# Cross attention: key and value sides made behind the first memory layer, scores in four banks

## The chip, the cores and the metric

The kernel runs on one core of a Trainium2 chip. The metric is the device time in microseconds from start to end of one execution; lower is better. TensorE is PE, VectorE is DVE, ScalarE is ACT, GpSimd is POOL, SyncE is SP.

## What is computed

Four batches of 256 tokens (width 256) pass four layers in a row: L0, a gated cross attention over a 1601 x 128 context with 16 heads of 64, and a GELU feed-forward; L1, a memory layer (attention over the same context, then a sigmoid gate and an RMS norm); L2, self attention, cross attention and an MLP; L3, a memory layer like L1. The part that the change touches is the cross attention of L2, 16 heads of 8:

```
cq = heads(rms_norm(hidden_states, ln_post_cross_w) @ cq_w, NH, CHD)
ck, cv = jnp.split(encoder_outputs @ ckv_w, 2, axis=-1)     # 1601 x 128 each, no dependence on x
cctx = sdpa(cq, heads(ck), heads(cv), causal=False)         # softmax(q k / sqrt(8)) v
hidden_states = hidden_states + cctx @ cdense_w
```

## The kernel before

The engines run written-out instruction streams, ordered by semaphores; there is no scheduler. Each engine loops over the four batches. Inside a batch: L0 pair by pair of heads, its output projection and feed-forward, `memory_layer(0)`, self attention, cross attention, MLP, `memory_layer(1)`. PE takes its instructions strictly in program order, so a wait ahead of one holds back all behind it.

PSUM has eight banks: `X[0]` and `X[1]` of two banks each, `ST[0]`, `ST[1]`, `PV`, `MI`. The 1664 padded keys are 13 tiles of 128 (`KT`), or two halves of 832 (`HALF`), each read as two pieces of 416 (`QUART`).

Cross attention of a batch. PE makes the queries in `MI`, then the keys of all heads in `X[0]` and `X[1]` (twice six matmuls of 416 columns; a factor is split into a high and a low part in fp32r). DVE splits queries and keys into high and low parts (`ck_hi`, `ck_lo`), clears the two `cq_blocks`, and writes the queries of a group into them (`queries`, L1462). The 16 heads go in four groups of four. For a group, `cross_stacks` (L1013, PE) spreads the four heads' keys over the partitions with a constant matrix, in `X[0]` and `X[1]`, and ACT (`keys`, L571) copies them to `ck_stack`, of which there are two. `cross_max` (L1030 on PE, L1472 on DVE) computes all scores of the group a first time, half a row at a time in `X[0]` or `X[1]`, 16 parts, and DVE reduces each to its maximum. The maxima of a row are negated, transposed by PE (`cross_shifts`) and written by DVE into four rows of `cq_blocks`, so that the second computation of the scores comes out shifted. That second one is the loop over the 13 key tiles: two scores matmuls of 512 columns into `ST[0]` and `ST[1]`, two exponentials on ACT into four slots of `probs` (L604), and `pv` (L1062), four matmuls of 32 output partitions, one tile behind. The stacks and the maxima of the next group lie between these on PE:

```
for kt in range(KT):
    for u in range(2):
        n = 2 * kt + u
        pe.wait_ge(pc_exp.handle, pc_exp.at(i, max(0, n - 1)))     # the exponential two back
        ...                                                        # scores n -> ST[n % 2]
    if gr < 3 and kt == 0:
        cross_stacks(gr + 1, 0); cross_stacks(gr + 1, 1)
    if gr < 3 and 1 <= kt < KT - 1:
        for n in range(...): cross_max(gr + 1, n)
    if kt:
        pv(kt - 1)
pv(KT - 1)
if gr < 3:
    cross_shifts(gr + 1)
```

Group 0 has no scores to lie beside: its 16 parts run alone, with the values (`cross_v`, L1001, 39 matmuls of 128 columns into `ST`, copied by ACT to `v_cross`) between them. `transposed(3)` sends 24 matmuls without a use (`WARM`, into `ST[0]`) ahead of the transposes that open self attention.

## Time and profile before

| | us |
|---|---|
| median of 3 runs (lowest, highest) | 2669.77 (2669.46, 2673.37) |
| the profiled execution, its own time | 2673.19 |
| its span, first to last instruction | 2671.4 |
| PE busy | 2186.9 (82% of the span) |
| DVE busy | 1571.4 (59%) |
| ACT busy | 851.5 (32%) |
| POOL busy | 467.8 (18%) |
| granted clock of PE, mean, as a share of 2.4 GHz | 0.887 |

A batch takes about 665 us. In the first one, L0 runs from 40 to 290 us, cross attention from 443 to 591 us. The timeline has one line for one or several equal instructions: start, length, engine, source line, operation, output and inputs, and in brackets how long the engine had been idle and who released it. L625 is PE's helper for every matmul and L1146 is DVE's for two-input operations, so the tiles' names tell the steps apart.

### The profile page before, as it was taken

To read this page: it belongs to the slowest core of one execution; us is meant where nothing else is said; L and a number is where in the kernel's file an instruction comes from. 1 tells how busy PE (TensorE), PEld (TensorE's weight loads), DVE (VectorE), ACT (ScalarE), POOL (GpSimd) and SP (SyncE) were. 2 spreads that over 40 slices of the span, in tenths; PEclk is the share of its full clock that TensorE was granted. 3 is DMA by queue.
4 is the path that set the end of the run, shared out by engine and by line. 5 is a ranking of instruction groups with operands and counts; after the bars stand their busy time and mean duration, and the time that the engine had idled before them with its cause. 6 is when DMAs were issued, how large, how long until landed. Compare 5 with 4: busy or idle time off the path is not lost.

```text
span 2671.4 us, 38462 instructions
## 1 busy us (share of the span) xinstructions
PE 2186.9 (82%) x12780; PEld 1616.3 (61%) x12780; DVE 1571.4 (59%) x2513; ACT 851.5 (32%) x1530; POOL 467.8 (18%) x412
## 2 busy tenths in 40 slices
PE   4999877888599978788859998868876999776987
PEld 3777665546477666554747766655464776665545
DVE  6777346653677735665377772566437776356643
ACT  2444111441244412044124441205412453120531
POOL 2444010000244401000034440100003443010000
PEclk7999887899699988799969998869896999986988
DMA  3000101001000010100100001010010000101000
GB/s 154 13 4 32 67 1 71 1 1 40 26 13 4 32 67 1 71 1 1 40 30 9 4 32 68 1 71 1 1 40 30 9 4 32 67 1 71 1 1 5
DMA packets 15567, 74.61 MB, mean 28 GB/s; under 512 B 2096, under 2 KB 3760, under 8 KB 11952
## 3 DMA queue, kind: packets, MB, share of 16 engines
q1 hardware_dynamic: 14256, 68.90, 6.9%
q10 hardware_dynamic: 1152, 3.67, 0.3%
q8 instruction: 90, 1.47, 0.2%
q14 instruction: 69, 0.57, 0.1%
HBM read 71.51 MB, written 1.05 MB: 27 GB/s over the span
## 4 chain that ended last, share of the span: by engine, by line
PE 72%; DVE 17%; issue 7%; ACT 3%; DMA 1%; POOL 0%; DVEq 0%; SPq 0%; ACTq 0%; POOLq 0%
PE x L625 26%; PE st L625 22%; PE pv L625 18%; PE mi L625 4%; DVE rstd_work L1146 1%; DVE prob_sums L1429 1%; DVE max_parts L1249 1%; PE x L646 1%; DVE k_hi_lo L1146 1%; DVE recip_sum L1300 1%; DVE cq_blocks L1484 1%; DVE rstd_work L1205 1%; ACT probs L510 1%; ACT k_hi_lo L468 1%; DVE max_parts L1476 1%
## 5 line engine op out<-in xcount | busy, mean ns | idle before, releaser
L510 ACT ACTIVATE probs<-st 128x512 f32<-128x512 f32 x416 | 229.6, 596 | 385.3 <-PE st L625 380.6
L1476 DVE TENSOR_REDUCE max_parts<-x 128x1 f32<-128x832 f32 x256 | 253.6, 1021 | 107.9 <-PE x L625 106.2
L1249 DVE TENSOR_REDUCE max_parts<-x 128x1 f32<-128x832 f32 x256 | 258.5, 1016 | 54.6 <-PE x L625 53.2
L604 ACT ACTIVATE probs<-st 128x512 f32<-128x512 f32 x416 | 226.4, 596 | 184.0 <-PE st L625 180.8
L625 PE MATMUL st<-q_hi_hi,k_hi_lo 128*128 128x256 f32 x832 | 236.9, 315 | 29.0 <-ACT v L476 14.3
L433 POOL TENSOR_TENSOR prob_sums<-prob_sums,probs 128x512 f32<-128x512 f32 x160 | 205.8, 1286 | 249.7 <-ACT probs L510 249.7
L625 PEld LDWEIGHTS st<-q_hi_hi,k_hi_lo 128*128 128x128 f32 x832 | 160.7, 193 | 104.2 <-issue 68.4
L625 PE MATMUL pv<-probs,v 128*64 128x256 f32 x1664 | 223.3, 393 | 0.0
L625 PE MATMUL st<-q_lo_shift,k_hi_rows 128*128 128x256 f32 x832 | 213.1, 287 | 0.0
L397 POOL TENSOR_SCALAR k_hi_rows<-probs,const_cols 64x1664 fp32r<-64x1664 f32 x16 | 26.4, 1660 | 991.0 <-DVE probs L1213 990.6
L1146 DVE TENSOR_TENSOR prob_sums<-prob_sums,probs 128x512 f32<-128x512 f32 (+1 forms) x168 | 155.1, 923 | 76.1 <-ACT probs L530 44.0
L625 PE MATMUL st<-cq_blocks,ck_stack 128*128 128x512 f32 x416 | 162.3, 466 | 32.1 <-DVE cq_blocks L1484 30.3
L625 PE MATMUL x<-ck_stack,cq_blocks 128*128 128x416 f32 x512 | 153.6, 416 | 29.1 <-DVE cq_blocks L1143 13.6
L1146 DVE TENSOR_TENSOR k_hi_lo<-x,k_hi_lo 64x832 fp32r<-64x832 f32 x128 | 130.9, 1023 | 73.6 <-ACT k_hi_lo L468 71.7
L625 PEld LDWEIGHTS st<-q_lo_shift,k_hi_rows 128*128 128x128 f32 x832 | 162.1, 195 | 0.0
L625 PE MATMUL x<-k_hi_rows,q_hi 128*128 128x416 f32 x512 | 144.0, 398 | 14.4 <-DVE max_parts L1249 12.0
L625 PEld LDWEIGHTS pv<-probs,v 128*64 128x64 f32 x1664 | 101.0, 137 | 77.2 <-ACT probs L510 24.3
L625 PEld LDWEIGHTS x<-ck_stack,cq_blocks 128*128 128x128 f32 x512 | 106.6, 221 | 62.0 <-issue 31.7
L625 PEld LDWEIGHTS st<-cq_blocks,ck_stack 128*128 128x128 f32 x416 | 68.5, 194 | 118.4 <-ACT probs L604 80.8
L646 PE MATMUL x<-const_f,x_normed 128*128 128x128 f32 x80 | 20.4, 405 | 145.9 <-DVE x_normed L1181 97.8
L625 PE MATMUL pv<-probs,v_cross 128*32 128x256 f32 x1664 | 138.6, 391 | 0.0
L468 ACT ACTIVATE k_hi_lo<-x 64x832 fp32r<-64x832 f32 x128 | 110.2, 861 | 26.5 <-PE x L625 24.0
(260 smaller groups left out, 4408.6 us busy)
## 6 DMA issues: line engine op xcount, KB each, us to landing
w_gate_up<-in_wgu SPq DMA_DIRECT2D x4, 3072.0 KB, 10.3
w_pair<-in_w SPq DMA_DIRECT2D x32, 256.0 KB, 2.6
w_ff<-in_w SPq DMA_DIRECT2D x8, 1024.0 KB, 5.8
w_qk<-in_wqk SPq DMA_DIRECT2D x4, 2048.0 KB, 8.9
w_down<-in_wdn SPq DMA_DIRECT2D x4, 1536.0 KB, 13.6
w_dense<-in_wd SPq DMA_DIRECT2D x4, 1024.0 KB, 12.2
mask_ints<-in_mask SPq DMA_DIRECT2D x4, 832.0 KB, 4.5
ctx_t_raw<-in_ctxT SPq DMA_DIRECT2D x4, 832.0 KB, 6.3
```

Source lines behind the costliest of these rows:

```text
L433: pool.tensor_tensor(acc[:, 0], acc[:, 0], prob[:, (2 * n + 2) % 4], ALU.add)\
L468: act.activation(t["kst"][0:64, h, j * HALF:(j + 1) * HALF].rearrange("p (c n) -> p c n", c=2), X[j][64 * h:64 * h + 64, :].rearrange("p ( ...
L510: act.activation(prob[:, kt % 4], ST[kt % 2][:], ACT.Exp, scale=HD0 ** -0.5).then_inc(p_exp.handle, 1)
L604: act.activation(prob[:, n % 4], ST[n % 2][:], ACT.Exp, scale=float(HC2) ** -0.5)\
L625: return pe.matmul(out, lhsT, rhs, start=start, stop=stop, skip_group_check=True)
L646: last = pe.transpose(X[0][:, o:o + P], src[:, t, ch * P:(ch + 1) * P], ident)
L1146: return dve.tensor_tensor(out, x, y, op)
L1205: link(dve.scalar_tensor_tensor(y, w, 1.5, y, ALU.add, ALU.mult))
L1249: dve.tensor_reduce(mxs[:, qt, h, half:half + 1], X[half][:].rearrange("p (c n) -> p c n", c=2)[:, :, 0:QUART], AX.XY, ALU.max).then_inc(m ...
L1300: dve.reciprocal(rec[:], PV[:, NT:2 * NT]).then_inc(recip.handle, 1)
L1429: link(dve.reciprocal(part, sums))
L1476: dve.tensor_reduce(mxs[:, qt, h, half:half + 1], X[half][:].rearrange("p (c n) -> p c n", c=2)[:, :, 0:QUART], AX.XY, ALU.max).then_inc(m ...
```

## The change

What it does, in the order of a batch:

- Behind the first memory layer PE makes the keys (`cross_k`), the values (`cross_v`) and the stacks of all four groups (`cross_stacks`, now in pieces of 512 columns, up to column 1602). ACT copies the keys twice (`ck_hi` and a full copy `ck`), POOL subtracts one from the other (`ck_lo`), ACT copies values and stacks. There are four `ck_stack` tiles. PE waits for all these copies before `transposed(3)`. The 24 filler matmuls there go.
- The weight `w_ckv` is loaded and split once, ahead of the loop. POOL clears `cq_blocks` and sets the padding columns; ACT writes the queries into `cq_blocks`.
- The maxima are computed by single banks of 512 columns: three per head and query tile, and one of 66 columns for four heads, 26 parts in place of 16. Group 0 takes four banks in turn, the others the two of `X[0]`.
- The scores use four banks (`ST[0]`, `ST[1]` and both of `X[1]`), the exponentials eight slots (`probs`, `probs_cross`). `pv` comes two key tiles at a time behind four scores. The shifts of the next group come ahead of the last `pv` calls. The values lie 16 columns apart, not 32.

PE's order behind the first memory layer, before (`x`, `mi`, `st`, `pv` are the PSUM tiles; out<-in, columns; REGISTER_ALU and ISA rows belong to waits):

```order
L625 MATMUL mi<-w_gate,mc_t 128x256 x2
L625 MATMUL st<-const_r 128x512 x24
L642 REGISTER_ALU
L646 MATMUL x<-const_f,x_normed 128x128 x4
L888 ISA
L625 MATMUL x<-x_v_t,w_qk 128x256 x2
```

And now, from the last stack (`cross_stacks(3, 1)`) on:

```order
L685 MATMUL x<-ck_hi,const_r 128x512
L685 MATMUL x<-ck_hi,const_r 128x258
L685 MATMUL x<-ck_lo,const_r 128x512
L685 MATMUL x<-ck_lo,const_r 128x258
L986 REGISTER_ALU
L702 REGISTER_ALU
L706 MATMUL x<-const_f,x_normed 128x128 x4
L991 ISA
L685 MATMUL x<-x_v_t,w_qk 128x256 x2
```

The filler gave way to the key, value and stack matmuls, whose last four are shown; the wait for the copies (L986) now stands ahead of the transposes.

PE's loop of a group with the next group's maxima, before: one key tile and the next.

```order
L625 MATMUL st<-cq_blocks_143,ck_stack_147 128x512
L1037 REGISTER_ALU
L625 MATMUL x<-ck_stack_148,cq_blocks_144 128x416 x2
L1037 REGISTER_ALU
L625 MATMUL x<-ck_stack_148,cq_blocks_144 128x416 x2
L625 MATMUL pv<-probs,v_cross 32x256 x4
L1077 REGISTER_ALU
L625 MATMUL st<-cq_blocks_143,ck_stack_147 128x512
```

The same place now:

```order
L685 MATMUL x<-ck_stack_156,cq_blocks_150 128x512
L1112 REGISTER_ALU
L685 MATMUL x<-ck_stack_156,cq_blocks_150 128x512
L685 MATMUL x<-cq_blocks_149,ck_stack_155 128x512
L1112 REGISTER_ALU
L685 MATMUL x<-ck_stack_156,cq_blocks_150 128x512
L685 MATMUL x<-cq_blocks_149,ck_stack_155 128x512
L1112 REGISTER_ALU
L685 MATMUL x<-ck_stack_156,cq_blocks_150 128x512
L685 MATMUL pv<-probs,v_cross 32x256 x8
L685 MATMUL st<-cq_blocks_149,ck_stack_155 128x512
```

Scores (`x` or `st` from `cq_blocks`) and single parts (`x` from the next `ck_stack`) alternate, and eight `pv` matmuls stand in a block where four stood. The diff, cut:

```diff
-WARM = {1: 12, 3: 24, 4: 12, 5: 12}
+WARM = {1: 12, 4: 12, 5: 12}
...
-        ks2 = [place(f"ck_stack{s}", [P, SK], F32R, e) for s in range(2)]
-        e = [max(c[0], e[0])]
+        ks2 = [place(f"ck_stack{s}", [P, SK], F32R, k) for s in range(4)]
+        vx = place("v_cross", [P, KT, (H2 + 1) * VXW], F32, k)
...
+            return X[k // 2][:, k % 2 * 512:k % 2 * 512 + 512]
+            return half_bank(m % (4 if gr == 0 else 2))
+            return (ST[0][:], ST[1][:], half_bank(2), half_bank(3))[n % 4]
+            return prob[:, n % 8] if n % 8 < 4 else prob2[:, n % 8 - 4]
...
+                pool.wait_ge(wo_mm.handle, wo_mm.at(b))
+                for n, (dst, value) in enumerate(((vx[:], 0.0), (vx[:].rearrange("p k (h d) -> p k h d", d=VXW)[:, :, :, HC2:HC2 + 1], 1.0))):
+                    pool.memset(dst, value).then_inc(vx_init.handle, 1)
...
+                for j in range(2):
+                    pool.wait_ge(kn_read.handle, kn_read.at(b, j + 1))
+                    pool.sem_inc(passed.handle, 1)
+                    c = slice(j * HALF, (j + 1) * HALF)
+                    pool.tensor_tensor(knl[:, c], knf[:, c], r32(knh[:, c]), ALU.subtract).then_inc(kn_low.handle, 1)
...
+                for k in range(2):
+                    pool.memset(r32(qb2[k][:]), 0.0).then_inc(qb_init.handle, 1)
...
+                def cross_k(j):
+                    act.wait_ge(ck_mm.handle, ck_mm.at(b, j + 1))
+                    x, c = X[j][:].rearrange("p (c n) -> p c n", c=2)[:, :, 0:QUART], slice(j * HALF, (j + 1) * HALF)
+                    act.activation(knh[:, c].rearrange("p (c n) -> p c n", c=2), x, ACT.Copy)
+                    act.activation(knf[:, c].rearrange("p (c n) -> p c n", c=2), x, ACT.Copy).then_inc(kn_read.handle, 1)
...
+                def cross_keys(gr, j):
+                    act.wait_ge(ks_mm.handle, ks_mm.at(b, 2 * gr + j + 1))
+                    n = HALF if j == 0 else S2 - HALF
+                    act.activation(ks2[gr][:, j * HALF:j * HALF + n], X[j][:, 0:n], ACT.Identity, bias=ck[:, K_OH_CROSS:K_OH_CROSS + 1])\
+                        .then_inc(ks_read.handle, 1)
+                act.wait_ge(vx_init.handle, vx_init.at(b))
+                cross_k(0)
+                cross_k(1)
+                cross_v(0)
+                cross_v(1)
+                for gr in range(4):
+                    cross_keys(gr, 0)
+                    cross_keys(gr, 1)
+                    if gr < 2:
+                        cross_v(gr + 2)
...
-                    for kt in range(KT):
-                        for u in range(2):
-                            n = 2 * kt + u
-                            act.wait_ge(sc_mm.handle, sc_mm.at(i, n + 1))
-                            act.wait_ge(pvc_mm.handle, pvc_mm.at(i, max(0, n - 3)))
-                            act.activation(prob[:, n % 4], ST[n % 2][:], ACT.Exp, scale=float(HC2) ** -0.5)\
-                                .then_inc(pc_exp.handle, 1)
-                        if gr < 3 and kt == 0:
-                            keys(i + 1, gr + 1, 0)
-                            keys(i + 1, gr + 1, 1)
+                    for n in range(2 * KT):
+                        act.wait_ge(sc_mm.handle, sc_mm.at(i, n + 1))
+                        act.wait_ge(pvc_mm.handle, pvc_mm.at(i, max(0, n - 7)))
+                        act.activation(slot(n), st_bank(n), ACT.Exp, scale=float(HC2) ** -0.5).then_inc(pc_exp.handle, 1)
+                        if gr < 3 and n == 1:
+                            cross_queries(gr + 1)
...
+                    if gr == 0:
+                        pe.wait_ge(kn_read.handle, kn_read.at(b, j + 1))
+                        pe.wait_ge(kn_low.handle, kn_low.at(b, j + 1))
+                    else:
+                        pe.wait_ge(ks_read.handle, ks_read.at(b, 2 * gr + j - 1))
+                    for n, x in enumerate((knh, knl)):
+                        for c0, c1 in ((0, 512), (512, HALF if j == 0 else S2 - HALF + 1)):
+                            m = mm(X[j][:, c0:c1], cr[:, R_CROSS + 4 * gr + n], x[:, j * HALF + c0:j * HALF + c1], n == 0, n == 1)
+                    m.then_inc(ks_mm.handle, 1)
+                cross_k(0)
+                pe.wait_ge(gz_ready.handle, gz_ready.at(b * 2))
+                cross_k(1)
+                cross_v(0)
+                cross_v(1)
+                for gr in range(4):
+                    cross_stacks(gr, 0)
+                    cross_stacks(gr, 1)
+                    if gr < 2:
+                        cross_v(gr + 2)
+                pe.wait_ge(ks_read.handle, ks_read.at(b))
+                pe.wait_ge(cv_read.handle, cv_read.at(b))
                 transposed(3, xn)
...
+                    i, banks, bank = b * 4 + gr, 4 if gr == 0 else 2, max_bank(gr, m)
+                    qt, h, c = m // 13, m % 13 // 3, m % 13 % 3
+                    if m == 0:
+                        pe.wait_ge(qg_read.handle, qg_read.at(i))
+                    if m >= banks:
+                        pe.wait_ge(mc2_read.handle, mc2_read.at(i, m - banks + 1))
+                    if m % 13 < 12:
+                        t = mm(bank, qb2[gr % 2][:, h, qt * P:(qt + 1) * P], ks2[gr][:, c * 512:(c + 1) * 512])
...
-                def cross_max(gr, n):
-                    i = b * 4 + gr
-                    half, h, qt = n % 2, n // 2 % 4, n // 8
-                    if n < 2:
-                        pe.wait_ge(ks_read.handle, ks_read.at(i))
...
-                    pe.wait_ge(mc2_read.handle, mc2_read.at(i, max(0, n - 1)))
-                    for ch in range(2):
-                        o = half * HALF + ch * QUART
-                        m = mm(X[half][:, ch * 512:ch * 512 + QUART], qb2[gr % 2][:, h, qt * P:(qt + 1) * P], ks2[gr % 2][:, o:o + QUART])
-                    m.then_inc(mc2_mm.handle, 1)
...
-                for j in range(2):
-                    cross_stacks(0, j)
...
-                for n in range(16):
-                    cross_max(0, n)
-                    if n % 4 == 1:
-                        cross_v(n // 4)
+                cross_queries(0)
+                for m in range(CPARTS):
+                    cross_max(0, m)
...
-                    if gr == 0:
-                        pe.wait_ge(cv_read.handle, cv_read.at(b))
...
-                                m = mm(PV[32 * hd:32 * hd + 32, 0:NT], vx[:, kt, 4 * gr + hd],
-                                       prob[:, n % 4, h * NT:(h + 1) * NT], kt == 0, kt == KT - 1)
+                                m = mm(PV[32 * hd:32 * hd + 32, 0:NT], vx[:, kt, VXW * (4 * gr + hd):VXW * (4 * gr + hd) + 32],
+                                       slot(n)[:, h * NT:(h + 1) * NT], kt == 0, kt == KT - 1)
...
-                    for kt in range(KT):
-                        for u in range(2):
-                            n = 2 * kt + u
-                            pe.wait_ge(pc_exp.handle, pc_exp.at(i, max(0, n - 1)))
-                            m = mm(ST[n % 2][:], ks2[gr % 2][:, kt * P:(kt + 1) * P],
-                                   qb2[gr % 2][:, 2 * u:2 * u + 2].rearrange("p h n -> p (h n)"))
-                            m.then_inc(sc_mm.handle, 1)
-                        if gr < 3 and kt == 0:
-                            cross_stacks(gr + 1, 0)
-                            cross_stacks(gr + 1, 1)
-                        if gr < 3 and 1 <= kt < KT - 1:
-                            for n in range((kt - 1) * 16 // (KT - 2), kt * 16 // (KT - 2)):
-                                cross_max(gr + 1, n)
-                        if gr == 3 and kt == 1:
+                    done_parts = 0
+                    for k0 in range(0, KT, 2):
+                        kts = range(k0, min(k0 + 2, KT))
+                        for kt in kts:
+                            for u in range(2):
+                                n = 2 * kt + u
+                                pe.wait_ge(pc_exp.handle, pc_exp.at(i, max(0, n - 3)))
+                                m = mm(st_bank(n), ks2[gr][:, kt * P:(kt + 1) * P],
+                                       qb2[gr % 2][:, 2 * u:2 * u + 2].rearrange("p h n -> p (h n)"))
+                                m.then_inc(sc_mm.handle, 1)
+                                if gr < 3:
+                                    if n == 1:
+                                        cross_queries(gr + 1)
+                                    while n > 1 and done_parts < min(CPARTS, (n - 1) * CPARTS // 20):
+                                        cross_max(gr + 1, done_parts)
+                                        done_parts += 1
+                        if k0 == 12 and gr < 3:
+                            cross_shifts(gr + 1)
+                        if gr == 3 and k0 == 4:
                             pe.wait_ge(cc_read.handle, cc_read.at(i - 1))
                             mm(X[0][:, 0:512], cc[:, C_SELC], cx[:, 0:2].rearrange("p k n -> p (k n)"))
                             mm(X[0][:, 512:512 + NT], cc[:, C_SELC], cx[:, 2]).then_inc(cc_sum.handle, 1)
-                        if kt:
-                            pv(kt - 1)
+                        if k0:
+                            pv(k0 - 2)
+                            pv(k0 - 1)
                     pv(KT - 1)
-                    if gr < 3:
-                        cross_shifts(gr + 1)
...
+            clink(dve.tensor_copy(wckh[:], wck[:]))
+            clink(tt(wckl[:], wck[:], r32(wckh[:]), ALU.subtract))
...
-                    for n in range(16):
-                        half, h, qt = n % 2, n // 2 % 4, n // 8
-                        dve.wait_ge(mc2_mm.handle, mc2_mm.at(b * 4 + gr, n + 1))
-                        dve.tensor_reduce(mxs[:, qt, h, half:half + 1], X[half][:].rearrange("p (c n) -> p c n", c=2)[:, :, 0:QUART],
-                                          AX.XY, ALU.max).then_inc(mc2_read.handle, 1)
+                    for m in range(CPARTS):
+                        qt, h, c, bank = m // 13, m % 13 // 3, m % 13 % 3, max_bank(gr, m)
+                        dve.wait_ge(mc2_mm.handle, mc2_mm.at(b * 4 + gr, m + 1))
+                        if m % 13 < 12:
+                            t = dve.tensor_reduce(mxc[:, qt, h, c:c + 1], bank, AX.X, ALU.max)
+                        else:
+                            t = dve.tensor_reduce(mxc[:, qt, :, 3], bank[:, 0:4 * HEADW].rearrange("p (h n) -> p h n", h=4), AX.X, ALU.max)
+                        t.then_inc(mc2_read.handle, 1)
...
```

The weights' DMA of `w_ckv` leaves the SP queue of a batch (five weight tensors in place of six) and is issued once ahead of the loop, with one more for the cosine and sine tables; `w_down` goes to another place in SBUF, issued at the same point.

## Rows read from the trace of the kernel before

**Rows 1.** The page, busy time of each engine over the span.
```profile
PE 2186.9 (82%) x12780; PEld 1616.3 (61%) x12780; DVE 1571.4 (59%) x2513; ACT 851.5 (32%) x1530; POOL 467.8 (18%) x412
```

**Rows 2.** Timeline of the first batch, from the split queries to group 0's first scores.
```profile
443.60 0.42 DVE L1146 TENSOR_TENSOR cq_lo<-mi,cq_hi 128x256 fp32r<-128x256 f32 x1
...
451.58 1.97 DVE L1143 TENSOR_SCALAR cq_blocks<-mi,const_cols 32x256 fp32r<-32x256 f32 x4
...
454.87 1.96 DVE L1476 TENSOR_REDUCE max_parts<-x 128x1 f32<-128x832 f32 x2 [1.33 <-PE x L625]
...
477.97 0.17 DVE L1479 TENSOR_REDUCE neg_max<-max_parts 128x8 f32<-128x16 f32 x1
...
480.54 1.21 PE L625 MATMUL st<-cq_blocks,ck_stack 128*128 128x512 f32 x2 [1.97 <-DVE cq_blocks L1484]
```

**Rows 3.** Timeline, one key tile of group 0 and the start of the next.
```profile
489.17 0.72 PE L625 MATMUL st<-cq_blocks,ck_stack 128*128 128x512 f32 x2
...
489.71 1.09 ACT L604 ACTIVATE probs<-st 128x512 f32<-128x512 f32 x2 [0.51 <-PE st L625]
489.74 0.92 PE L625 MATMUL x<-ck_stack,cq_blocks 128*128 128x416 f32 x4
490.32 3.01 DVE L1476 TENSOR_REDUCE max_parts<-x 128x1 f32<-128x832 f32 x3 [0.58 <-PE x L625]
...
490.59 0.64 PE L625 MATMUL pv<-probs,v_cross 128*32 128x256 f32 x8
...
491.16 0.72 PE L625 MATMUL st<-cq_blocks,ck_stack 128*128 128x512 f32 x2
```

**Rows 4.** Timeline: first scores of group 1, then of group 3, its sums, its last `pv`.
```profile
510.09 0.97 PE L625 MATMUL st<-cq_blocks,ck_stack 128*128 128x512 f32 x2 [1.87 <-DVE cq_blocks L1484]
...
566.84 0.73 PE L625 MATMUL st<-cq_blocks,ck_stack 128*128 128x512 f32 x2 [1.87 <-DVE cq_blocks L1484]
...
569.10 2.77 PE L625 MATMUL x<-ctx_heads_t,const_f 128*128 128x512 f32 x4
...
586.39 1.64 PE L625 MATMUL pv<-probs,v_cross 128*32 128x256 f32 x16
```

**Rows 5.** Groups by line and form: busy us, mean ns of one, idle before.
```profile
L1476 DVE TENSOR_REDUCE max_parts<-x 128x1 f32<-128x832 f32 x256 | 253.6, 1021 | 107.9 <-PE x L625 106.2
...
L1333 DVE TENSOR_REDUCE max_parts<-x 128x1 f32<-128x416 f32 x16 | 9.3, 580 | 0.0
...
L578 ACT ACTIVATE ck_stack<-x,const_cols 128x832 fp32r<-128x832 f32 x16 | 15.3, 956 | 148.9 <-PE x L625 148.3
L550 ACT ACTIVATE k_stack<-mi,const_cols 128x256 fp32r<-128x256 f32 x32 | 15.2, 475 | 37.3 <-PE mi L625 37.3
...
L594 ACT ACTIVATE v_cross<-st 128x512 f32<-128x512 f32 x12 | 7.2, 597 | 71.5 <-PE st L625 71.5
...
L433 POOL TENSOR_TENSOR prob_sums<-prob_sums,probs 128x512 f32<-128x512 f32 x160 | 205.8, 1286 | 249.7 <-ACT probs L510 249.7
```

**Rows 6.** Timeline of the first batch, from the first memory layer's gate to self attention.
```profile
343.09 5.84 PE L625 MATMUL st<-const_r 128*128 128x512 f32 x24
...
344.27 0.63 ACT L535 ACTIVATE gate_tanh<-gate_in 128x512 f32<-128x512 f32 x1 [4.51 <-DVE gate_in L1146]
...
355.60 1.11 PE L646 MATMUL x<-const_f,x_normed 128*128 128x128 f32 x4 [6.68 <-DVE x_normed L1179]
...
359.21 2.07 PE L625 MATMUL x<-x_v_t,w_qk 128*128 128x256 f32 x4 [2.49 <-DVE x_l_t L1146]
```

**Rows 7.** Windows: stretch, length, busy of PE, PEld, DVE, ACT, POOL; PEclk, DMA share, GB/s.
```profile
310.00:318.00 8.00, 4.38 (x18) 2.36 (x16) 5.16 (x9) 1.67 (x2) 0.00 (x0) 1.00 0.00 0
...
361.00:363.00 2.00, 2.00 (x6) 1.56 (x5) 0.00 (x0) 0.00 (x0) 2.00 (x1) 0.50 0.00 0
461.00:463.00 2.00, 2.00 (x9) 1.97 (x10) 1.95 (x2) 0.00 (x0) 0.00 (x0) 0.50 0.00 0
487.00:508.00 21.00, 21.00 (x159) 11.16 (x158) 16.09 (x17) 12.17 (x23) 0.00 (x0) 1.00 0.01 2
```

194 lines of the change are left out of this document (90 added, 104 removed).

## The prediction

> **What bounds the kernel now.** The page first: PE is busy 82% of the span, DVE 59%, ACT 32% [rows 1]. A share over the span settles nothing for an edit to one stage, so the cross attention was read from the timeline of the first batch, in three pieces.
>
> The opening lasts from the split queries (end of `cq_lo`, 443.60 + 0.42 = 444.02) to group 0's first scores at 480.54: 36.5 us without a score or an exponential [rows 2]. DVE clears `cq_blocks` and writes the queries until 453.55, the first reduction starts at 454.87, the last ends at about 477.95. PE puts 39 value matmuls between the parts, and a bank pair has to be emptied before it is filled.
>
> The groups with maxima beside them: group 0 starts at 480.54, group 1 at 510.09, group 3 at 566.84 [rows 2, 4], so group 0 takes 29.55 us and groups 1 and 2 take 28.4 each. A key tile with four parts' matmuls takes 491.16 - 489.17 = 1.99 us: two scores 0.57, four maxima matmuls of 416 columns 0.85, `pv` 0.57 [rows 3]. They follow one another without a hole: PE bounds this loop, ACT has 1.09 us of exponentials in it.
>
> Group 3 has no maxima. It ends with its last `pv`, 586.39 + 1.64 = 588.03: 21.2 us [rows 4].
>
> At the place that the work moves to, PE has done the gate matmuls of the memory layer at 343.09, runs filler, then sits idle for 6.68 us until the transposes at 355.60 [rows 6].
>
> The profiled execution took 2673.2 us, 3.4 above the median of 2669.8. The sum is made against the first and shifted by that.
>
> **Opening.** Removed: the clearing and the queries on DVE, the keys' split, the values between the parts. What is left after 444.02: two matmuls for the queries 0.5, hand-over to ACT 0.3 (a score starts at 489.17, its exponential at 489.71, and its own matmul is about 0.23), four writes on ACT at 0.475 [rows 5], which overlap a little as the two exponentials in 1.09 do: 1.7, and 0.6 from the first maxima matmul to its reduction (489.74 to 490.32) [rows 3]. That is 3.2 with a wait of 0.1. Then DVE reduces. A reduction of 832 columns takes 1.021, of 416 0.580 [rows 5]: 1.06 ns a column, so 512 columns take 0.68 alone. Back to back two of 832 take 1.96, 0.08 less than twice 1.021 [rows 2], so I take 0.65, and 0.40 for the part of 264 columns. 24 x 0.65 + 2 x 0.40 = 16.4. PE needs 0.23 a part (24 matmuls of 512 columns in 5.84 [rows 6] are 0.24), or 0.46 at the lower clock, and has four banks, so DVE bounds it at either. The way from the last reduction to the scores stays: 477.97 to 480.54, 2.6 [rows 2]. Sum 22.2 against 36.5: **-14.3 us a batch**. At 0.68 a part and every hand-over 0.1 longer it is -13.
>
> **Groups 0 to 2.** Work per group: PE 26 scores and 24 parts at 0.23, eight short matmuls under 0.1, 13 `pv` at 0.57, about 20 us; DVE 16.4, plus about 2.3 for the shifts and a copy; ACT 26 x 0.55 + 1.7 = 16. No engine fills 28 us, so the order decides. I walk it. Two scores and the queries' matmuls end at 0.95. ACT has its two exponentials first and then the four writes, done at about 3.1. PE stands at the first part until then, DVE starts at 3.5. From here DVE needs 16.4, but PE puts a block of eight `pv` (1.14, and about 0.24 for the two switches of kind, since 0.57 is more than two scores' 0.46) four times between parts, with a score behind it. DVE holds two banks at most at that point, one just begun: 1.3 us. PE returns with a new part after 1.38 + 0.23 + 0.23 and 0.3 of hand-over, about 2.2. Hole: 0.9 to 1.4, one a block, and small ones at the short parts: 4.5 in all. DVE ends at 24.4, the last part left PE at 23.8. Behind it PE has four scores 0.9, three blocks' worth of `pv` (tiles 8 and 9, then 10 to 12) 3.1 and the transposes, with a short wait for DVE, 0.5. DVE's writes of the shifts hide beside the last three `pv`; before, PE was idle 1.87 there [rows 4]. Sum **28.3**, against 28.4. What the deeper buffers and the hidden shifts give, the holes at the `pv` blocks and the late queries take. Group 0 starts behind a stretch in which PE is half idle and will run its first microseconds at the lower level, as now; I leave its 1.1 more. 3 x 28.3 + 1.1 = 86.0 against 86.3: **-0.3**. Bounds per group: 26, if the holes go, and 29.6, if each change between score and part costs PE 0.05.
>
> **Group 3.** 26 exponentials at 0.55 are 14.3, 0.5 ahead, 0.9 behind. The sums of `ctx_heads_t` (2.77 us [rows 4], taken as at the lower clock; 1.4 at the upper) stand with a `pv` block ahead of the next scores: 1.4 + 1.4 + 0.5 against 2.2 of exponentials in four banks, 1.1 lost. 16.8 against 21.2: **-4.4**.
>
> **Behind the memory layer.** ACT is free at 344.9. Two copies of 0.956 for each half of the keys [rows 5] end at 348.7, two values of 0.597 at 350.0. POOL subtracts 832 columns: from 1.286 for 512 [rows 5], 2.1 each, done at 349.1 and 351.3. Stacks cost PE 0.76 (1664 columns at the rate above). The first two copies end at 351.2 and 353.3, the third value at 353.9. Six copies are left, and a bank pair goes round in 0.92 copy + 0.1 + 0.76 + 0.25 = 2.03 for two copies: 6.1. The transposes start at 360.1 in place of 355.6: **+4.5**. The ends: ACT's 13.3 us without a wait, +2.9; stacks at the lower clock, +7.5. The `x_normed` they used to wait for is hidden by this; if the copies were shorter, it would be next. POOL's fills come ahead of the wait and have no reader near. The SP queue loses a small transfer.
>
> Before, the first matmuls of self attention run at half the clock: granted 0.50 from 361 to 363 behind the idle stretch [rows 6, 7]. At the upper level they would save up to 2.2 us. PE will now be 60% busy ahead of them, and 310 to 318 shows 55% busy at a clock of 1.00 [rows 7]. But the gap ahead of 359.21, for which DVE prepares `x_v_t`, stays. I take half: **-1.1**. The Trainium skill ("TensorE: Matmul & The Clock Gate", section "Why this matters for your kernels") says that idle gaps between bursts of matmuls bring the lower level back; going by it alone, this term would be the whole -2.2, and the total 4 us lower.
>
> **Sum.** -14.3 - 0.3 - 4.4 + 4.5 - 1.1 = -15.6 a batch, -62.4 for four, +0.8 for two operations of the split ahead of the loop: 2673.2 - 61.6 = 2611.6, as a median 2608.
>
> **Rivals.** *The holes close* (0.20). PE finds the next part's bank free sooner than I walk it, and a group takes 26. For it: DVE has 9 us of slack in a group. Against: PE's order is fixed. 12 groups x 2.3: 2580.
>
> *Everything moved costs more* (0.19). Alternating single matmuls cost PE a little each (29.6 a group, +16) and the stacks run at the lower clock with POOL late (+12): 2636. For it: a tile's three kinds take 0.57 + 0.85 + 0.57 although their columns need less.
>
> *The clock stays low* (0.07), the one that ends slower. Place: groups 0 to 2. PE now waits there for DVE part by part. At half the clock its 20 us become 40, and a group is PE-bound at about 40: 12 x 12 more, 2752. It turns slower once PE spends 43% of these groups low (62 of 144). For it: from 461 to 463 the clock stays at 0.50 although PE is busy throughout [rows 7]. Against: 487 to 508 holds 1.00, 310 to 318 holds 1.00 at 55% busy [rows 7], and at the lower level PE would have no holes at all. The Trainium skill (same page, section "A second HAM failure mode: psum-queue depth-cycling") reports this for another kernel: small idle pieces while cycling through PSUM banks make the clock swing. By that rule this rival would be the forecast; the rows at 1.00 with holes speak against it.
>
> *The change doesn't do what it says* (0.02): the wait for the copies (L986) grows as long as the opening shrank, as when POOL's subtractions take 6 us each. No change.
>
> **How the numbers follow.** My forecast has 0.52. The range 2576 to 2650 takes in the first two rivals and the bounds of the terms, and leaves out the clock rival and the tails. Measurements of this kernel agree within about 0.2%, 5 us. Faster 0.91, same 0.02, slower 0.07.
>
> **What would show it.** Right: 22 us from `cq_lo` to the first scores, reductions of 0.65 to 0.68 without holes in it; group starts 28 apart, with four holes of about 1 us on DVE; group 3 about 17; transposes near 360, released by ACT's last `ck_stack`; a clock of 1.00 in the groups. Wrong: a clock of 0.5 beyond a group's first microseconds, groups outside 26 to 30, or transposes after 364.

## The result and the profile after

The changed kernel takes 2642.8 us (median of 4 runs, 2640.5 to 2644.3) against 2671.6 for the kernel before: ratio 0.9891, 95% interval 0.9874 to 0.9908. The forecast was a change of -61.6 us; measured is -28.8. The sign and the range (2576 to 2650) held, the size did not.

Both profiles were cut at the same six DVE instructions of each batch: the first of the batch, `h_t` (input of the feed-forward part), the first `gate_in` (end of the first memory layer's matmuls), `x_v_t` (start of self attention), the end of `cq_lo`, and the second `x_v_t` (behind cross attention). "Forecast" is my sum of four batches, sorted into these stages; the clock's -1.1 a batch falls into self attention.

| us, four batches | before | after | change | forecast |
|---|---|---|---|---|
| ahead of the first batch | 21.1 | 22.8 | +1.7 | +0.8 |
| batch start to `h_t` | 1085.6 | 1089.7 | +4.0 | 0 |
| `h_t` to `gate_in` | 201.2 | 213.7 | **+12.6** | 0 |
| `gate_in` to `x_v_t` | 56.5 | 77.3 | +20.8 | +18.0 |
| `x_v_t` to `cq_lo` (self attention) | 345.0 | 346.5 | +1.5 | -4.4 |
| `cq_lo` to second `x_v_t` (cross attention) | 641.5 | 570.6 | **-70.9** | -76.0 |
| rest | 320.5 | 321.2 | +0.7 | 0 |
| span | 2671.4 | 2641.8 | -29.6 | -61.6 |

Cross attention gave 93% of what was forecast. Of the 32.0 us that the span misses, 16.6 were lost ahead of `gate_in`, where the forecast had zero. The gain differs by batch: measured between the stores of the result, the first two batches gain 10 and 12 us, the last two 4 and 3.

Of the page, the row of busy times (before: [rows 1]):

```profile
PE 2169.6 (82%) x12684; PEld 1584.7 (60%) x12684; DVE 1539.0 (58%) x2579; ACT 889.3 (34%) x1578; POOL 486.7 (18%) x444
```

The shares are the same to 2 points: they don't tell which stages gained and which lost.

**Cross attention of the first batch** (timeline of the changed kernel, PE and DVE; columns as in [rows 2]):

```profile
450.68 0.42 DVE L1222 TENSOR_TENSOR cq_lo<-mi,cq_hi 128x256 fp32r<-128x256 f32 x1
...
469.99 0.18 DVE L1536 TENSOR_REDUCE neg_max<-max_cross 128x8 f32<-128x32 f32 x1
...
472.61 1.22 PE L685 MATMUL st<-cq_blocks,ck_stack 128*128 128x512 f32 x2 [1.79 <-DVE cq_blocks L1541]
...
502.56 0.73 PE L685 MATMUL st<-cq_blocks,ck_stack 128*128 128x512 f32 x2 [0.36 <-DVE cq_blocks L1541]
...
506.16 0.50 PE L685 MATMUL x<-ck_stack,cq_blocks 128*128 128x512 f32 x1 [2.40 <-ACT cq_blocks L657]
...
531.29 0.73 PE L685 MATMUL st<-cq_blocks,ck_stack 128*128 128x512 f32 x2 [0.36 <-DVE cq_blocks L1541]
...
560.57 0.73 PE L685 MATMUL st<-cq_blocks,ck_stack 128*128 128x512 f32 x2 [0.36 <-DVE cq_blocks L1541]
...
576.03 0.75 PE L685 MATMUL pv<-probs,v_cross 128*32 128x256 f32 x8
```

The opening is 472.61 - 451.10 = 21.5 us (36.5 before [rows 2]; forecast 22.2): 3.7 to the first reduction, 15.1 of reductions, 2.7 behind them. Groups 0 to 2 take 29.95, 28.73 and 29.28, together 88.0 (86.3 before; forecast 86.0). Group 3 takes 16.2 (21.2 before [rows 4]; forecast 16.8). Behind their first scores groups 1 and 2 have 2.40 us in which PE waits for ACT's query writes, group 0 has 1.82.

DVE in group 0, whose reductions are of 0.65 us back to back, has the four holes of the walk, at the blocks of `pv` (eight matmuls of the program, which the trace records as 16):

```profile
483.56 3.25 DVE L1531 TENSOR_REDUCE max_cross<-x 128x1 f32<-128x512 f32 x5 [0.86 <-PE x L685]
...
488.52 3.25 DVE L1531 TENSOR_REDUCE max_cross<-x 128x1 f32<-128x512 f32 x5 [1.23 <-PE x L685]
492.73 3.26 DVE L1531 TENSOR_REDUCE max_cross<-x 128x1 f32<-128x512 f32 x5 [0.96 <-PE x L685]
496.97 1.29 DVE L1531 TENSOR_REDUCE max_cross<-x 128x1 f32<-128x512 f32 x2 [0.97 <-PE x L685]
```

**Behind the memory layer** (first batch) the transposes start at 363.42, released by ACT's last `ck_stack` as forecast (before: 355.60 [rows 6]); 3.6 us of the difference had come in ahead of it, with the gate matmuls:

```profile
350.17 3.88 POOL L483 TENSOR_TENSOR ck_lo<-ck,ck_hi 128x832 fp32r<-128x832 f32 x2 [57.37 <-ACT ck L590]
...
351.15 0.99 DVE L1222 TENSOR_TENSOR rstd_work<-mean_var 128x2 f32<-128x2 f32 x1
...
352.18 1.88 DVE L1274 SCALAR_TENSOR_TENSOR rstd_work<-rstd_work,mean_var 128x2 f32<-128x2 f32 x1
...
363.42 0.65 PE L706 MATMUL x<-const_f,x_normed 128*128 128x128 f32 x4 [1.32 <-ACT ck_stack L604]
```

Two steps of DVE on 2 columns take 0.99 and 1.88 us in place of 0.16, and the second ends with the second of POOL's subtractions (350.17 + 3.88 = 354.05). Here this costs nothing: `x_normed` is ready at 361.67, 1.5 us ahead of ACT's last copy.

**Ahead of `h_t`** (third batch) the same happens with POOL's fill of `v_cross`. DVE's step and PE's transposes before the change:

```profile
1613.76 0.17 DVE L1143 TENSOR_SCALAR rstd_work<-mean_var 128x2 f32<-128x2 f32 x1
...
1617.26 0.66 PE L646 MATMUL x<-const_f,x_normed 128*128 128x128 f32 x4 [2.87 <-DVE x_normed L1181]
```

POOL, DVE and PE of the changed kernel:

```profile
1589.29 3.06 POOL L473 MEMSET v_cross<- 128x3536 f32 x1 [12.57 <-PE x L685]
...
1590.07 0.75 DVE L1266 BATCH_NORM_STATS2 bn_stats<-x_b 128x6 f32<-128x256 f32 x2
...
1591.26 1.11 DVE L1219 TENSOR_SCALAR rstd_work<-mean_var 128x2 f32<-128x2 f32 x1
...
1592.48 0.52 DVE L1278 TENSOR_SCALAR rstd_work<-rstd_work 128x2 int32<-128x2 int32 x1
1592.50 0.48 POOL L473 MEMSET v_cross<- 128x221 f32 x1 [0.15 <-POOL v_cross L473]
...
1596.14 1.12 PE L706 MATMUL x<-const_f,x_normed 128*128 128x128 f32 x4 [4.24 <-DVE x_normed L1259]
```

The first `rstd_work` step lasts until the fill is over (1589.29 + 3.06 = 1592.35). PE's idle time ahead of the transposes is 4.24 us, before the change 2.87.

**The clock by stage** (windows of the third batch, before; then after. Stretch, length, busy time of PE, PEld, DVE, ACT, POOL, then the granted clock, DMA share, GB/s):

```profile
1618.00:1668.10 50.10, 41.44 (x190) 34.57 (x191) 14.25 (x24) 8.28 (x12) 0.00 (x0) 0.90 0.12 50
1668.10:1682.20 14.10, 6.47 (x28) 4.78 (x26) 10.77 (x46) 0.63 (x1) 1.50 (x4) 0.84 0.01 2
...
1768.40:1928.80 160.40, 135.46 (x783) 81.81 (x781) 99.42 (x138) 68.33 (x125) 0.00 (x0) 0.86 0.02 7
```

```profile
1597.30:1651.40 54.10, 46.04 (x190) 37.51 (x191) 14.38 (x24) 8.28 (x12) 0.00 (x0) 0.78 0.07 29
1651.40:1672.20 20.80, 16.87 (x87) 14.57 (x85) 13.36 (x46) 12.66 (x17) 6.81 (x10) 0.84 0.01 1
...
1759.20:1902.70 143.50, 120.72 (x702) 65.87 (x702) 87.77 (x155) 65.94 (x121) 0.00 (x0) 0.84 0.02 8
```

From `h_t` to `gate_in` PE has the same 190 matmuls, but needs 46.04 us of busy time in place of 41.44, and the mean clock is 0.78 in place of 0.90. Nothing of this stage was edited. The first batch loses less here than the other three: 51.5 us at 0.86, where the kernel before had 50.9 at 0.87.

### The profile page after: what moved, and what is told of

Read it like the earlier page. It is cut to its first block, busy times and chain, and to the rows that moved or that the text cites. A ratio compares the mean times of both kernels' runs of the same rounds, so it can differ in the third digit from the quotient of the medians.

```text
span 2641.8 us, 38249 instructions
## 1 busy us (share of the span) xinstructions
PE 2169.6 (82%) x12684; PEld 1584.7 (60%) x12684; DVE 1539.0 (58%) x2579; ACT 889.3 (34%) x1578; POOL 486.7 (18%) x444
## 4 chain that ended last, share of the span: by engine, by line
PE 64%; DVE 21%; issue 9%; ACT 4%; POOL 1%; DMA 1%; DVEq 0%; SPq 0%; ACTq 0%; POOLq 0%
PE x L685 26%; PE pv L685 16%; PE st L685 15%; PE mi L685 4%; DVE max_cross L1531 3%; DVE k_hi_lo L1222 2%; DVE max_parts L1327 2%; DVE recip_sum L1378 2%; DVE prob_sums L1507 1%; ACT k_hi_lo L514 1%; DVE rstd_work L1222 1%; ACT cq_blocks L657 1%; PE x L706 1%; DVE cq_blocks L1541 1%; DVE rstd_work L1283 1%
## 5 line engine op out<-in xcount | busy, mean ns | idle before, releaser
L556 ACT ACTIVATE probs<-st 128x512 f32<-128x512 f32 x416 | 229.7, 596 | 386.5 <-PE st L685 381.6
L1531 DVE TENSOR_REDUCE max_cross<-x 128x1 f32<-128x512 f32 x384 | 247.2, 685 | 120.6 <-PE x L685 119.6
L1327 DVE TENSOR_REDUCE max_parts<-x 128x1 f32<-128x832 f32 x256 | 258.5, 1017 | 54.8 <-PE x L685 54.4
L685 PE MATMUL x<-ck_stack,cq_blocks 128*128 128x512 f32 (+1 forms) x512 | 213.8, 490 | 50.6 <-ACT cq_blocks L657 34.7
L685 PE MATMUL x<-k_hi_rows,q_hi 128*128 128x416 f32 x512 | 143.2, 395 | 15.8 <-DVE max_parts L1327 12.6
L685 PEld LDWEIGHTS pv<-probs,v 128*64 128x64 f32 x1664 | 100.8, 136 | 76.9 <-ACT probs L556 24.4
L666 ACT ACTIVATE probs<-st 128x512 f32<-128x512 f32 x128 | 70.8, 595 | 144.0 <-PE st L685 142.0
L685 PE MATMUL st<-w_pair_hi,ctx_t_hi 128*128 128x128 f32 x416 | 114.3, 275 | 2.8 <-ACT v L522 2.8
L685 PE MATMUL st<-w_pair_lo,ctx_t_hi 128*128 128x128 f32 x416 | 114.6, 275 | 0.0
L685 PEld LDWEIGHTS x<-k_hi_rows,q_hi 128*128 128x128 f32 x512 | 88.4, 204 | 43.4 <-DVE max_parts L1327 39.7
```

Of the source, the lines that this page charges most:

```text
L556: act.activation(prob[:, kt % 4], ST[kt % 2][:], ACT.Exp, scale=HD0 ** -0.5).then_inc(p_exp.handle, 1)
L666: act.activation(slot(n), st_bank(n), ACT.Exp, scale=float(HC2) ** -0.5).then_inc(pc_exp.handle, 1)
L685: return pe.matmul(out, lhsT, rhs, start=start, stop=stop, skip_group_check=True)
L1327: dve.tensor_reduce(mxs[:, qt, h, half:half + 1], X[half][:].rearrange("p (c n) -> p c n", c=2)[:, :, 0:QUART], AX.XY, ALU.max).then_inc(m ...
L1531: t = dve.tensor_reduce(mxc[:, qt, h, c:c + 1], bank, AX.X, ALU.max)
```

## The experiments

Each edit is against the changed kernel unless said otherwise. All ratios are to the kernel before the change, on the same chip. The table has the stages of the third batch, so that the runs can be compared; its numbers come from the timelines, cut as above. The median of the kernel before was 2671.6 to 2674.5 us from one set of runs to the next, so a difference in us between two rows is good to some 3 us.

| run | median us | to `h_t` | to `gate_in` | to `x_v_t` | to `cq_lo` | to second `x_v_t` |
|---|---|---|---|---|---|---|
| before | 2671.6 | 271.5 | 50.1 | 14.1 | 86.2 | 160.4 |
| the change | 2642.8 | 273.0 | 54.1 | 20.8 | 87.0 | 143.5 |
| fills behind `h_t` | 2622.3 | 271.8 | 51.8 | 17.9 | 89.4 | 141.9 |
| no low part | 2624.1 | 269.8 | 54.1 | 16.2 | 85.5 | 143.1 |
| `pv` by single tiles | 2672.9 | 269.9 | 54.2 | 20.7 | 87.4 | 149.7 |
| queries ahead | 2604.7 | 270.0 | 54.1 | 20.8 | 87.4 | 132.7 |
| three banks each | 2616.4 | 271.1 | 53.9 | 20.8 | 87.4 | 135.5 |
| more filler ahead of `h_t` | 2635.9 | 269.5 | 51.1 | 20.8 | 87.3 | 143.4 |
| fills, queries, banks | 2551.8 | 268.5 | 51.9 | 17.8 | 86.0 | 124.4 |
| the same with filler in four gaps | 2515.3 | 271.8 | 48.1 | 17.9 | 81.9 | 125.3 |
| before, fill alone moved | 2698.6 | 275.8 | 51.3 | 14.2 | 87.0 | 160.3 |
| before, with filler | 2645.1 | 269.9 | 50.1 | 14.1 | 83.3 | 157.4 |
| the change, with filler | 2595.6 | 271.1 | 52.6 | 17.8 | 82.6 | 139.8 |

### Where the time ahead of cross attention went

**The fills behind `h_t`.**

```diff
-                pool.wait_ge(wo_mm.handle, wo_mm.at(b))
+                pool.wait_ge(xt_read.handle, xt_read.at(b, 2))
```

> Theory: POOL's fill of v_cross (3.06 us) and its small ones now run beside DVE's normalisation ahead of h_t, and DVE's short rstd_work steps wait for POOL (one of them 1.11 us in place of 0.17); h_t is 1.4 us late, PE idles longer, and the clock of TensorE falls behind it, which costs the memory layer 4 us in three batches. With the fills behind h_t, where DVE is idle: h_t back by 1.4 a batch, h_t to gate_in back from 54.1 to 50.1 in batches 1 to 3, perhaps the stacks' 2.9 us in batches 2 and 3 too: 2617 to 2625. Rival: the low clock there has another cause; then only 1.4 a batch come back: 2637.

Measured: 2622.3 us, ratio 0.981 (0.9794 to 0.9827), 20 us less than the change. DVE and POOL of the third batch:

```profile
1586.07 0.17 DVE L1219 TENSOR_SCALAR rstd_work<-mean_var 128x2 f32<-128x2 f32 x1
...
1591.88 3.04 POOL L473 MEMSET v_cross<- 128x3536 f32 x1 [20.38 <-DVE h_t L1219]
```

The step is back at 0.17 us, and `h_t` to `gate_in` falls from 54.1 to 51.8, not to 50.1. The next stage is 17.9 us at a clock of 1.00 in every batch. So the first theory holds for the fills, with the clock coming back by half. New is self attention at 89.4 us in three batches, 85.2 in the first: what the clock gave in one stage, it took in part in the next. Over four batches, against the change, the stages give 5.5 us (to `h_t`), 8.4, 5.9, -6.9 and 3.9: DVE's wait itself, 1.3 us a batch, is the smaller part of the 20 us, the clock behind it the larger.

**The same fill, moved in the kernel before the change.**

```diff
+                pool.wait_ge(wo_mm.handle, wo_mm.at(b))
+                pool.sem_inc(passed.handle, 1)
+                for n, (dst, value) in enumerate(((vx[:], 0.0), (vx[:, :, :, HC2:HC2 + 1], 1.0))):
+                    pool.memset(dst, value).then_inc(cross_init.handle, 1)
...
                 pool.wait_ge(gate_mm.handle, gate_mm.at(b * 2))
...
-                for s, steps in ((self_init, inits), (cross_init, [(vx[:], 0.0), (vx[:, :, :, HC2:HC2 + 1], 1.0)])):
+                for s, steps in ((self_init, inits),):
```

> The kernel before the change, with nothing else than POOL's fill of v_cross (5.65 us there) moved to where the change has it, behind the output projection. Theory: DVE's rstd_work steps wait for the fill, h_t comes 3.5 to 4 us later, the clock falls behind it, and h_t to gate_in goes from 50.1 to 54.1: 7.5 us a batch, about 2702. Rival: no reader is near, as the prediction had it: 2672.

Measured: 2698.6 us, ratio 1.0091 (1.0074 to 1.0108): 24.5 us slower than the 2674.1 of its set, from moving fills that nobody nearby reads. The fill is longer here, 6656 columns for the change's 3536. POOL and DVE, third batch:

```profile
1625.23 5.66 POOL L444 MEMSET v_cross<- 128x6656 f32 x1 [12.48 <-PE x L631]
```

```profile
1627.20 3.71 DVE L1149 TENSOR_SCALAR rstd_work<-mean_var 128x2 f32<-128x2 f32 x1
```

A step on two columns takes 3.71 us and ends at 1630.91; the fill ends at 1630.89. `h_t` comes 4.3 us later (275.8 for 271.5), a little more than expected, and the stages behind it lose 1.2 and 0.8, not the 4 expected. PE idles 6.74 us ahead of the transposes (2.87 without the move). The wait is as the theory has it; its price in clock was put too high for this kernel.

**More filler ahead of `h_t`, the fills left where they are.**

```diff
-WARM = {1: 12, 4: 12, 5: 12}
+WARM = {1: 24, 4: 12, 5: 12}
```

> 24 filler matmuls in place of 12 ahead of the transposes for h_t; POOL's fills stay where the change has them. Theory: the memory layer's 4 us (h_t to gate_in 54.1 for 50.1) come from the clock, which falls because PE idles 4.2 us in place of 2.9 ahead of those transposes; filler that reaches to 1 us before them keeps it up, at no cost: h_t to gate_in back to 50.1, h_t itself still 1.4 us late: 2626 to 2631. Rival: the 4 us are something else (weights or operands late); then nothing or a loss: 2642 to 2650.

Measured: 2635.9 us, ratio 0.986 (0.9843 to 0.9877), 5 us above the upper end of what was expected. PE of the third batch:

```profile
1589.82 5.82 PE L685 MATMUL st<-const_r 128*128 128x512 f32 x24
1597.19 0.66 PE L706 MATMUL x<-const_f,x_normed 128*128 128x128 f32 x4 [1.54 <-DVE x_normed L1259]
```

The idle time is 1.54 us in place of 4.24, the transposes take 0.66 in place of 1.12, and `h_t` to `gate_in` is 51.2 in all four batches (54.1 in three of the changed kernel's). DVE's step beside the fill still takes 1.11 us, so 2.9 of the 4 us are the clock alone. But the next stage is now 20.8 in all four batches, where the changed kernel had 17.9 in two: about 6 us given back.

**No low part of the keys.** The subtraction is left out, and in the stacks the high part stands for it, so this kernel computes its scores from altered keys.

```diff
-                    pool.tensor_tensor(knl[:, c], knf[:, c], r32(knh[:, c]), ALU.subtract).then_inc(kn_low.handle, 1)
...
-                        pe.wait_ge(kn_low.handle, kn_low.at(b, j + 1))
-                    for n, x in enumerate((knh, knl)):
+                    for n, x in enumerate((knh, knh)):
```

> The low part of the keys is left out (POOL subtracts nothing, PE multiplies the high part twice, so PE's work is the same). Theory: POOL's two subtractions hold back DVE's rstd_work steps (0.99 and 1.88 us) and PE's first stacks: x_normed 2.5 us earlier against the gate, the transposes 1.3 us earlier (PE's idle 0.37 and 0.91 ahead of the first two stacks goes, ACT's last copy still ends last), 2637 without a change of clock, down to 2625 if the stacks of batches 2 and 3 keep the upper level. Rival: ACT's copies alone set this stretch, nothing moves but x_normed: 2642.

Measured: 2624.1 us, ratio 0.9818 (0.9801 to 0.9834). `gate_in` to `x_v_t` is 16.1 to 16.2 in every batch: 1.7 less than 17.9, where 1.3 was expected, and the batches at 20.8 are gone. DVE and then PE, third batch:

```profile
1652.17 0.16 DVE L1216 TENSOR_TENSOR rstd_work<-mean_var 128x2 f32<-128x2 f32 x1
1652.37 0.16 DVE L1268 SCALAR_TENSOR_TENSOR rstd_work<-rstd_work,mean_var 128x2 f32<-128x2 f32 x1
```

```profile
1662.72 0.65 PE L701 MATMUL x<-const_f,x_normed 128*128 128x128 f32 x4 [1.31 <-ACT ck_stack L599]
```

DVE's two steps are back at 0.16 and 0.16 from 0.99 and 1.88, so it was POOL that held them. That wait was not what cost time, though: ACT, which stood still for 0.78 and 0.90 us ahead of its first two stacks while PE waited for the low part, now waits 0.21. The transposes still wait for ACT's last copy, which comes sooner because its stacks do: ACT's copies set this stage, 2 us above the kernel before.

### What sets a group's length

**Queries ahead.**

```diff
                 cross_queries(0)
+                cross_queries(1)
...
-                        if gr < 3 and n == 1:
-                            cross_queries(gr + 1)
+                    if gr < 2:
+                        cross_queries(gr + 2)
...
-                        m = pe.transpose(MI[0:4, NT + qt * P:NT + (qt + 1) * P], nmx[:, qt, :], ident)
+                        m = pe.transpose(X[0][0:4, qt * P:(qt + 1) * P], nmx[:, qt, :], ident)
```

> The queries of group gr + 2 are made behind the last score of group gr (those of group 1 in the opening), and the shifts' transposes go to X[0] in place of MI, so that they share no bank with the queries that ACT reads. Theory: PE's 2.5 us without work at a group's start and DVE's first reduction 4.2 us into the group were the late queries; from cq_lo to the second x_v_t it takes 134 us in place of 141.8 to 143.5, the clock no longer drops at the starts of groups 1 and 2, in all about 2607. Rival: the tail of a group (scores, pv and transposes behind the last part) sets its length: groups stay at 28 and more, 2635.

Measured: 2604.7 us, ratio 0.9735 (0.971 to 0.976), as the theory had it. Group 1's start on DVE (first batch):

```profile
506.53 0.42 DVE L1558 COPY ctx_heads_t<-pv 128x256 f32<-128x256 f32 x1
507.81 4.53 DVE L1534 TENSOR_REDUCE max_cross<-x 128x1 f32<-128x512 f32 x7 [0.85 <-PE x L686]
```

The first reduction starts 1.25 us into the group (506.56), not 4.1, and the shift writes, which end a group, lie 27.3, 26.0 and 25.8 us apart in this batch (30.0, 28.7, 29.3 in the change). The clock is at 1.00 throughout groups 1 and 2 of every batch.

Lengths of groups are best compared where the clock is the same. From shift write to shift write, at a clock of 1.00 throughout, a group takes 27.6 us in the kernel before, 28.7 in the change and 26.0 here.

**Three banks each.**

```diff
-            return half_bank(m % (4 if gr == 0 else 2))
+            return half_bank(m % (4 if gr == 0 else 3))
-            return (ST[0][:], ST[1][:], half_bank(2), half_bank(3))[n % 4]
+            return (ST[0][:], ST[1][:], half_bank(3))[n % 3]
...
-                                pe.wait_ge(pc_exp.handle, pc_exp.at(i, max(0, n - 3)))
+                                pe.wait_ge(pc_exp.handle, pc_exp.at(i, max(0, n - 2)))
```

> In the groups, three banks for the maxima and three for the scores in place of two and four. Theory: DVE's holes of 0.9 to 1.2 us at the pv blocks are there because two banks hold 1.3 us of reductions and a block of 16 pv with its neighbours keeps PE away longer; with three banks (1.95 us) they are gone, and a group takes about 26.5: 2614. Rival: what DVE gains, the group waits for elsewhere (its order is tied to the scores, and they now wait for the exponentials three back): 2640.

Measured: 2616.4 us, ratio 0.9785 (0.976 to 0.9811). DVE in group 1 of the first batch:

```profile
514.07 3.08 DVE L1531 TENSOR_REDUCE max_cross<-x 128x1 f32<-128x512 f32 x5 [0.98 <-PE x L685]
...
518.35 3.08 DVE L1531 TENSOR_REDUCE max_cross<-x 128x1 f32<-128x512 f32 x5 [0.86 <-PE x L685]
521.90 3.08 DVE L1531 TENSOR_REDUCE max_cross<-x 128x1 f32<-128x512 f32 x5 [0.47 <-PE x L685]
525.44 1.29 DVE L1531 TENSOR_REDUCE max_cross<-x 128x1 f32<-128x512 f32 x2 [0.46 <-PE x L685]
```

The time is what the theory gave, the mechanism only in part: two holes shrank to 0.47 and 0.46, two stand at 0.98 and 0.86. From its shift write to the next, this group takes 26.3 us (28.7). The 0.98 follows a short stretch at the lower clock; in the next group, at 1.00 throughout, the holes are 0.47, 0.86, 0.47 and 0.46, and it takes 25.3 us. The holes were not gone, as the theory had it, but about halved.

**`pv` by single tiles.**

```diff
-                    for k0 in range(0, KT, 2):
-                        kts = range(k0, min(k0 + 2, KT))
+                    for k0 in range(KT):
+                        kts = range(k0, k0 + 1)
...
-                            pv(k0 - 2)
```

> Each key tile's pv stands behind that tile's scores, in twelve blocks of four matmuls in place of six of eight; four score banks, eight slots and single-bank maxima as in the change. Theory: the blocks of eight cause DVE's holes of 0.9 to 1.2 us; with blocks of four they shrink below 0.4 and a group takes about 27: 2625. Rival: each change of kind costs PE time, and PE bounds the group: 29.6 and more, 2655.

Measured: 2672.9 us, ratio 0.9992 (0.998 to 1.0004). The theory is wrong and the rival near: 30 us more than the change, all of its gain. DVE in the group that starts at 506.9, first batch:

```profile
517.73 1.29 DVE L1530 TENSOR_REDUCE max_cross<-x 128x1 f32<-128x512 f32 x2 [1.12 <-PE x L685]
519.43 1.98 DVE L1530 TENSOR_REDUCE max_cross<-x 128x1 f32<-128x512 f32 x3 [0.41 <-PE x L685]
...
524.59 1.29 DVE L1530 TENSOR_REDUCE max_cross<-x 128x1 f32<-128x512 f32 x2 [0.79 <-PE x L685]
```

The holes are shorter, but there is one at nearly every tile: nine of 0.4 us and more add to 6.2 us in this group, against 4.2 in the four of the same group in the change, and the group takes 32.0 us (28.7). Part of this is the clock, which was at 0.50 from 511 to 517 here and at 1.00 throughout in the change. The next group, at 1.00 throughout, has nine holes of 4.6 us in all and takes 29.5 us. So at the same clock single tiles cost 0.8 us a group, some 9 us for the twelve (an estimate); the rest of the 30 goes with more and longer stretches at the lower clock, here and outside cross attention (which has 25.5 of the 30). A block of 16 recorded `pv` keeps PE 1.01 us (515.42 to the next score at 516.43 in the changed kernel), two of eight keep it 2 x 0.57. So shorter absences of PE in greater number gave nothing; how much of their cost is the hand-over to DVE and how much the switch on PE was not separated.

### Together, and with the clock held up

**Fills, queries and banks.** The three edits above.

> Fills behind h_t, queries ahead and three banks each, together. Theory: 20 us from the fills as measured alone, and with PE and DVE both fed a group takes 23.5 to 24.5 in place of 28.9 to 30.3: 2557 to 2570. Rival: queries and banks remove the same wait, so that they don't add up: 2587.

Measured: 2551.8 us, ratio 0.9554 (0.9537 to 0.9572). Against the change, the edits alone gave 20, 38 and 26 us; together 91, at least the sum (the intervals leave open whether it is more) and 5 us beyond what was expected. The shift writes of the first batch lie 24.4, 22.8 and 22.5 us apart. Cross attention of the third batch (windows, columns as above):

```profile
1712.50:1836.90 124.40, 108.81 (x702) 61.58 (x702) 84.64 (x156) 64.06 (x121) 0.00 (x0) 0.93 0.03 11
```

The clock is 0.93 where it was 0.84. At a clock of 1.00 a group takes 22.8 us: the 2.7 of the queries and the 3.4 of the banks come off the 28.7 nearly in full. PE is busy for 22.2 us of it (24.5 of 28.7 in the change): it is now what bounds the groups.

**Filler in four gaps on top of it.**

```diff
-WARM = {1: 12, 4: 12, 5: 12}
+WARM = {1: 20, 4: 12, 5: 12}
...
+                    warm(7)
                     pe.wait_ge(pc_ready.handle, pc_ready.at(i))
...
                 transposed(3, xn)
+                warm(8)
...
+                warm(22)
                 pe.wait_ge(cxm_ready.handle, cxm_ready.at(b))
```

> The kernel of the fills, the queries and the banks together, with filler matmuls in four more of PE's gaps: 8 more ahead of the transposes for h_t, 7 ahead of pc_t in both memory layers, 8 between the transposes of x_normed and w_qk, 22 ahead of the dense matmuls. Theory: each of these gaps of 2.3 to 6.7 us is followed by 3 to 8 us at clock 0.50, in which PE is the bound; with PE busy up to 0.5 us before the work the level stays at 1.00: 2 us each, five places, 8 to 10 a batch, 2512 to 2520. Rival: the level falls with or without filler, or the filler itself runs late; then 2552 or up to 10 us more.

Measured: 2515.3 us, ratio 0.9414 (0.9392 to 0.9435), the fastest of this study, 5.9% below the kernel before. The dense matmuls behind the gap of 6.69 us, third batch, without and with the filler:

```profile
1692.51 3.78 PE L686 MATMUL x<-w_dense,ctx_v_t 128*128 128x256 f32 x8 [6.69 <-DVE ctx_l_t L1225]
```

```profile
1659.09 5.60 PE L686 MATMUL st<-const_r 128*128 128x512 f32 x22
1666.36 1.99 PE L686 MATMUL x<-w_dense,ctx_v_t 128*128 128x256 f32 x8 [1.67 <-DVE ctx_l_t L1231]
```

The same eight matmuls take 1.99 us in place of 3.78. Self attention goes from 89.4 and 86.0 to 81.6 - 82.0.

**The same filler in the kernel before, and in the change.**

> The kernel before the change with filler in the same four gaps as the run before last. Theory: the filler's gain is not tied to the change's stages; 36 us were measured on top of the three edits, here 30 to 36: 2637 to 2643. Rival: before the change the level was up in most of these places, and the filler gives under 15: 2658 and more.

> The changed kernel with the same filler. Theory: with the clock held up, the change's losses ahead of gate_in and behind the copies go (h_t to gate_in near 50, the x_v_t stretch 17.9 in every batch), only the wait of DVE for the fill stays: 2585 to 2595, that is 48 us ahead of the kernel before with filler, in place of 29 without. Rival: the filler gives both kernels the same: 2606 to 2612.

Measured: 2645.1 us, ratio 0.9892 (0.9876 to 0.9909), and 2595.6 us, ratio 0.9709 (0.9693 to 0.9725). For the kernel before the result lies 2 us above what was expected, for the change just above its range. Filler gives the one 29 us, the other 47, and with filler in both the change is worth 49.5 us in place of 28.8. The mean granted clock of the profiled executions rises from 0.887 to 0.903 in the one and from 0.886 to 0.912 in the other. As filler computes nothing, about 20 of the missing 33 us are put down to the clock, behind gaps that the change had lengthened or shifted. That is a difference of differences, good to some 7 us by the intervals. The filler did not hold the clock up everywhere either: in the changed kernel `h_t` to `gate_in` took 50.1 us in two batches and 52.5 in the other two, at a mean clock of 0.81.

## Why the forecast was half right

- **Opening** (-14.3 a batch): 21.5 us for 22.2. Right; of its steps, DVE starts 3.7 us in (3.2 forecast), the reductions take 15.1 (16.4) because they follow one another every 0.60 us and not 0.65, and 2.7 lie behind them (2.6).
- **Groups 0 to 2** (-0.3): 88.0 for 86.0 in the first batch. The holes of the walk (0.9 to 1.4) measured 0.86, 1.23, 0.96 and 0.97. Two things were too small. ACT starts its four writes 1.6 us into the group and takes 1.90 (they start 0.48 apart and do not overlap, where I let them overlap a little), so that in groups 1 and 2 the first part follows at 3.6 and DVE at 4.1, where I had 3.1 and 3.5. And the clock, on both sides. The 28.4 that I took for groups 1 and 2 before the change is the mean of 29.1, with a stretch at the lower level, and of 27.6 at 1.00 throughout. Against the 27.6 the changed kernel's 28.7 at 1.00 is a loss of 1.1. And in the third and fourth batch PE's 2.40 us without work are followed by low stretches in groups 1 and 2 (third batch, below), which the first batch has in group 2 only:

```profile
1814.00:1819.00 5.00, 4.65 (x12) 2.57 (x12) 3.72 (x6) 3.09 (x6) 0.00 (x0) 0.68 0.00 0
1844.00:1849.00 5.00, 5.00 (x12) 3.10 (x12) 3.77 (x6) 2.67 (x5) 0.00 (x0) 0.50 0.00 0
```

- **Group 3** (-4.4): 16.2 us for 16.8. Right.
- **Behind the memory layer** (+4.5): +3.8 in two batches and +6.7 in two. ACT's last copy ends it, as walked, and POOL's subtraction takes 1.9 for the 2.1 taken. That `x_normed` is hidden by this held too (it is ready at 361.67 in the first batch, ACT's last copy at 363.15). Not seen was that POOL holds DVE up, which is harmless here, and that half of the batches run this stage at a mean clock of 0.84, for which +7.5 had been the outer end.
- **The clock in self attention** (-1.1): +0.4, which over four batches is 5.9 us worse than forecast. PE at work ahead of the gap did not keep the level up behind it; the gap right ahead of the matmuls stayed (2.50 us), and the granted clock was 0.53 from 1672.1 to 1677.1 (third batch). The sentence set beside this term, from the Trainium skill ("TensorE: Matmul & The Clock Gate", section "Why this matters for your kernels"), agrees with that, idle gaps bring the lower level back; it was my reading of it, that busy stretches ahead of the gap would spare 2.2 us, that was wrong.
- **The step that failed** is "POOL's fills come ahead of the wait and have no reader near", with the zero for everything ahead of `gate_in` that rested on it. The fill has no reader near, but DVE's short steps next to it stand still until it ends. Measured, the two stages ahead of `gate_in` cost 4.0 and 12.6 us. Moved back to where DVE is idle the fill gives 20 us; moved alone in the kernel before it costs 24.5. In the change the wait itself is 1.3 us a batch and the larger part comes through the clock: PE's idle time grows with the wait (4.24 us for 2.87), and the clock is lower behind it. In the kernel before, with the longer fill, the wait itself is most of it (275.8 for 271.5 us ahead of `h_t`). The Trainium skill ("SBUF — State Buffer", section "Who interferes with whom") has GpSimd and VectorE share a port pair that one of them holds for a whole instruction, and names the VectorE instructions that need it: those with two inputs in SBUF beside a GpSimd instruction that reads SBUF, and copies, casts and `tensor_scalar` in their two-port modes. The rows agree. Beside the subtractions two-input steps take 1.88 and 0.99 us for 0.16, beside the fills `TENSOR_SCALAR` steps take 3.71 and 1.11 for 0.17 (their mode does not show in the trace), each up to the end of POOL's instruction, while the statistics just before, with one input in SBUF, kept their 0.75.
- **The missing rival** is a clock that drops behind gaps outside cross attention. I had the clock as a rival for groups 0 to 2 alone and gave it 0.07 as the slower outcome. It neither halved the groups nor stayed away: it took up to 4 us a batch in the memory layer, 2.9 behind the stacks and 0.7 to 1.1 at a group's start. Beside the small holes between banks, which that rival was about, the clock stayed at 1.00 (500.81 to 529.53 in the first batch).
- Of the rivals, *the holes close* did not happen, and *everything moved costs more* comes close to the time (2636) for partly other reasons: the stacks at the lower clock in half of the batches, but no 0.05 us for each change of kind (at 1.00, scores and parts that alternate start 0.23 to 0.24 us apart). Its 29.6 us a group is near the measured 28.7 to 30.3, which came from the late queries and the clock.

What stays open: which stage of a batch runs low. The same stage takes 50.1, 51.2, 51.8 or 54.1 us (`h_t` to `gate_in`), 17.9 or 20.8 (to `x_v_t`), 85.2 to 89.4 (to `cq_lo`) with the same instructions, and an edit in one of them changes the others. The clock goes with the length each time (0.90, 0.87, 0.85 and 0.78 for the first four, 1.00 and 0.84 for the next two), and also in the batch's first stage, which with the fill in the same place takes 270.0 us at 0.93 in some kernels and 273.0 at 0.91 in the change (third batch). What decides it, no run shows.

## What to carry to other kernels

Cost a moved POOL instruction by what DVE does beside it, not by its readers: put it where DVE waits for PE. When a stage is shortened or an instruction moved, list PE's gaps (2.3 to 6.7 us where filler was put here) and what runs behind each; filler that ended 1.5 to 1.7 us ahead of the next matmul delayed nothing, and in four gaps was worth 29 to 47 us here. Compare the lengths of a stage where the clock is the same. And where two engines hand single banks to each other, give the waiting side a third bank (26 us here) and make its operands a round ahead (38 us) before tuning the order.

## What the runs showed of the hardware that was not expected

- A fill by POOL (3.06 or 5.66 us, writing SBUF only) and its two subtractions (1.9 us each) held up DVE instructions on two columns until their own end: 1.11, 3.71, 0.99 and 1.88 us in place of 0.16 to 0.17.
- The same eight dense matmuls took 3.78 us behind 6.69 us of idle time and 1.99 behind filler and 1.67; the level did not fall over that gap. Behind a gap of 1.54 us (more filler ahead of `h_t`) the transposes ran at the upper level too, but the clock was 0.50 from 1598.5 to 1601.5, right behind them.
- Effects of the clock do not add up by stage: 2.9 us won a batch in one stage (more filler ahead of `h_t`) came with 2.9 lost in the next in two batches of four.
